# Row broadcasts as transposes, half of batch 0's weight quantising on VectorE, and new orders ahead of the experts

## The reference

```python
def _smooth_quant_linear(x, w):
    amax_x = jnp.max(jnp.abs(x), axis=0)
    amax_w = jnp.max(jnp.abs(w), axis=0)
    s = jnp.maximum(jnp.sqrt(jnp.maximum(amax_x, EPS) / jnp.maximum(amax_w, EPS)), EPS)
    xs, ws = x / s, w * s
    x_scale = jnp.maximum(jnp.max(jnp.abs(xs), axis=-1, keepdims=True), EPS) / QMAX
    w_scale = jnp.maximum(jnp.max(jnp.abs(ws), axis=-1, keepdims=True), EPS) / QMAX
    x_q = jnp.clip(jnp.round(xs / x_scale), -QMAX, QMAX)
    w_q = jnp.clip(jnp.round(ws / w_scale), -QMAX, QMAX)
    return x_q @ w_q.T * x_scale * w_scale.T
...
h = _smooth_quant_linear(xe, guw)                  # first layer "a"
gate, up = jnp.split(h, 2, axis=-1)
a = jax.nn.silu(gate) * up
return _smooth_quant_linear(a, dw)                 # second layer "b"
...
x = x + jnp.tanh(g_xattn[0]) * xattn(_layernorm(x), ...)
x = x + jnp.tanh(g_ffn[0]) * moe(_layernorm(x), ...)   # top 2 of 16, plus shared expert
```

## Time and profile before

| | us |
|---|---|
| median of 3 runs | 571.96 (571.3 to 572.04) |
| profiled execution | 572.15 |
| its span, first to last instruction | 570.1 |
| TensorE busy | 541.2 (95%) |
| VectorE busy | 419.4 (74%) |
| ScalarE busy | 331.3 (58%) |
| GpSimd busy | 155.4 (27%) |

### The profile page before, as it was taken

How to read it: one execution, slowest core, us unless ns; L and a number is a source line. 1 busy time by engine, 2 the same in 40 slices (tenths; PEclk the granted TensorE clock), 3 DMA queues, 4 the chain that set the end, 5 groups by cost and what they waited for, 6 DMA issues and landing times.

```text
span 570.1 us, 10175 instructions
## 1 busy us (share of the span) xinstructions
PE 541.2 (95%) x3768; PEld 459.9 (81%) x3776; DVE 419.4 (74%) x828; ACT 331.3 (58%) x570; POOL 155.4 (27%) x187
## 2 busy tenths in 40 slices
PE   7897879999999999999999999999999999999997
PEld 3453438986888788888889999999999999999985
DVE  3777988998899786587576666666666667765785
ACT  3286776686648627423466666666666667752221
POOL 3428790431033101103222111111111100066730
PEclk9989999999999999999999999999999999999999
DMA  7940121013001130113877776666677767556862
GB/s 265 386 145 2 37 107 43 2 38 147 1 2 38 75 102 2 68 57 88 270 254 251 254 241 225 226 225 225 228 237 254 247 216 249 176 160 188 261 216 75
DMA packets 45891, 89.52 MB, mean 157 GB/s; under 512 B 4304, under 2 KB 24784, under 8 KB 44832
## 3 DMA queue, kind: packets, MB, share of 16 engines
q1 hardware_dynamic: 40736, 72.26, 37.8%
q0 software_dynamic: 5120, 16.78, 9.2%
HBM read 72.25 MB, written 16.78 MB: 156 GB/s over the span
## 4 chain that ended last, share of the span: by engine, by line
PE 57%; DVE 23%; ACT 8%; POOL 6%; issue 5%; DMA 1%; DVEq 0%; SPq 0%; POOLq 0%; ACTq 0%
PE ps_gu L1866 9%; PE ps_gu L1867 9%; PE ps_gu L1868 9%; PE ps_d L1866 6%; PE ps_d L1868 5%; PE ps_d L1867 5%; PE ps_a L2120 3%; POOL w L492 2%; POOL sw_lo L508 2%; PE ps_gu L2427 1%; DVE bn_b L1101 1%; PE ps_d L1887 1%; DMA raw_gu<-in_L_ffn_w_up 1%; ACT y L760 1%; DVE x L1323 1%
## 5 line engine op out<-in xcount | busy, mean ns | idle before, releaser
L1866 PE MATMUL ps_gu<-ex_xhi,w_hi 128*128 128x256 f32 x352 | 99.5, 283 | 0.7 <-DVE wb L1461 0.5
L1867 PE MATMUL ps_gu<-ex_xlo,w_hi 128*128 128x256 f32 x352 | 99.5, 283 | 0.0
L1868 PE MATMUL ps_gu<-ex_xhi,w_lo 128*128 128x256 f32 x352 | 99.4, 282 | 0.0
L1866 PEld LDWEIGHTS ps_gu<-ex_xhi,w_hi 128*128 128x128 f32 x352 | 67.0, 190 | 3.3 <-issue 0.9
L1867 PEld LDWEIGHTS ps_gu<-ex_xlo,w_hi 128*128 128x128 f32 x352 | 67.1, 191 | 1.7
L1004 ACT ACTIVATE ex_hhi<-ex_hid 128x256 fp32r<-128x256 f32 (+1 forms) x66 | 27.6, 418 | 68.3 <-DVE ex_hid L1724 67.3
L1868 PEld LDWEIGHTS ps_gu<-ex_xhi,w_lo 128*128 128x128 f32 x352 | 67.1, 191 | 0.0
L1866 PE MATMUL ps_gu<-xt_hi,sw_hi 128*128 128x256 f32 x220 | 65.1, 296 | 0.1
L1867 PE MATMUL ps_gu<-xt_lo,sw_hi 128*128 128x256 f32 x220 | 62.0, 282 | 0.0
L1868 PE MATMUL ps_gu<-xt_hi,sw_lo 128*128 128x256 f32 x220 | 62.0, 282 | 0.0
L1866 PE MATMUL ps_d<-wd_hi,ex_hhi 128*128 128x512 f32 (+1 forms) x132 | 54.2, 411 | 1.4 <-DVE ex_hlo L1726 1.0
(11 more groups left out here) (255 smaller groups left out, 1386.7 us busy)
## 6 DMA issues: line engine op xcount, KB each, us to landing
raw_gu<-in_L_ffn_w_gate SPq DMA_DIRECT2D x16, 704.0 KB, 4.4
raw_gu<-in_L_ffn_w_up SPq DMA_DIRECT2D x16, 704.0 KB, 5.9
raw_d<-in_L_ffn_w_down SPq DMA_DIRECT2D x16, 512.0 KB, 7.2
expert_out_scratch<-eo SPq DMA_DIRECT2D x16, 512.0 KB, 7.3
w<-in_fside_BxS2xS SPq DMA_DIRECT2D x4, 1024.0 KB, 5.4
x2n_scratch<-y SPq DMA_DIRECT2D x4, 1024.0 KB, 3.9
x<-in_x SPq DMA_DIRECT2D x1, 3072.0 KB, 16.4
raw_d<-in_L_ffn_w_down SPq DMA_DIRECT2D x16, 192.0 KB, 7.3
```

The source lines that it names most:

```text
L1866: pe.matmul(dst, a_hi, b_hi, start=start, stop=False)
L1867: pe.matmul(dst, a_hi, b_lo, start=False, stop=False)
L1868: return pe.matmul(dst, a_lo, b_hi, start=False, stop=stop)
```

## The change

`row` uses four fp32 transposes instead of four fp32 matmuls. Batch 0's `quant_w` becomes `quant_w_first` on ScalarE (the first two groups of rows) and `quant_w_rest` on VectorE (the other two), with a semaphore of its own that `turn_qw(0, ...)` also waits for. All five lists have a new order ahead of the experts, and the fillers other counts. The same calls are made otherwise. The diff, cut to its core:

```diff
@@ SyncE
             load_w2(2)
+            store_x2n(1)
             load_w1(3)
-            store_x2n(1)
             load_w2(3)
@@ GpSimd
             scale_w(0)
+            norm_a(1)
+            norm_a(2)
             split_gu_lo(0)
-            norm_a(1)
-            split_gu_lo(1)
-            norm_a(2)
             root_b(0)
             scale_w2(0)
             root_a(1)
-            split_gu_lo(2)
             scale_w(1)
             split_d_lo(0)
+            split_gu_lo(1)
             norm_b(0)
             split_d_lo(1)
+            split_gu_lo(2)
             split_gu_lo(3)
@@ ScalarE
+            def quant_w_first(a):
+                act.wait_ge(w_steps_done[LA], a + 1)
+                for j in range(HALF):
+                    last = act.activation(w1[:, j, :], w1[:, j, :], ACT.Copy, bias=MAGIC + LOW16, scale=small[LA]["w_inv"][:, j:j + 1])
+                last.then_inc(qw_done[LA], 1)
...
             normalise_a(0)
-            tanh()
             copy_s(0)
             quant_x(0)
             ints_x(0, 0)
-            quant_w(0)
+            quant_w_first(0)
             ints_x(0, 1)
             copy_w(0)
             ints_w(0, 0)
             ints_w(0, 1)
+            split_d_hi(0)
             split_gu_hi(0)
             split_gu_hi(1)
-            router()
-            split_d_hi(0)
             silu_a(0)
             abs_w(1)
             normalise_a(1)
             abs_x(1)
             split_gu_hi(2)
             copy_sb(0)
+            tanh()
+            split_gu_hi(3)
             quant_g(0)
+            router()
+            copy_s(1)
+            ints_g(0)
             quant_w2(0)
-            ints_g(0)
             copy_wb(0)
-            copy_s(1)
             ints_w2(0)
             quant_x(1)
...
@@ VectorE
+            def quant_w_rest(a):
+                dve.wait_ge(w_steps_done[LA], a + 1)
+                for j in range(HALF, J):
+                    last = dve.tensor_scalar(w1[:, j, :], w1[:, j, :], small[LA]["w_inv"][:, j:j + 1], MAGIC + LOW16, ALU.mult, ALU.add)
+                last.then_inc(qw_rest_done, 1)
...
             w_steps(0)
+            quant_w_rest(0)
             stats_a(1)
+            amax_w2(0, 1)
             stats_a(2)
-            amax_w2(0, 1)
             dequant_a(0, 0)
...
             x_steps(1)
+            router()
+            w_steps(1)
             dequant_b(0, 0)
             dequant_b(0, 1)
             dequant_b(0, 2)
             dequant_b(0, 3)
-            w_steps(1)
             add_x(0)
             stats_b(0)
+            dequant_a(1, 0)
             stats_a(3)
...
@@ TensorE
             def row(dst, cols):
                 for c in range(C):
-                    last = pe.matmul(dst[:, c * P:(c + 1) * P], cols[:, c:c + 1].broadcast_to((P, P)), ident[:], start=True, stop=True)
+                    last = pe.transpose(dst[:, c * P:(c + 1) * P], cols[:, c:c + 1].broadcast_to((P, P)), ident[:])
...
                 pe.wait_ge(qw_done[LA], a + 1)
+                if a == 0:
+                    pe.wait_ge(qw_rest_done, 1)
...
             row_s(0)
-            keep_busy(23)
+            turn_w2(0, 1)
+            turn_router()
+            keep_busy(21)
             turn_qx(0, 0)
-            turn_router()
             turn_qx(0, 1)
+            keep_busy(1)
             row_w(0)
-            keep_busy(8)
+            keep_busy(6)
             turn_qw(0, 0)
-            turn_w2(0, 1)
             turn_qw(0, 1)
-            keep_busy(4)
+            keep_busy(5)
             product_a(0, 0)
...
             row_rs(1)
             keep_busy(1)
+            row_s(1)
             turn_qg(0)
             row_w2(0)
-            row_s(1)
+            keep_busy(8)
             turn_qw2(0)
...
             table(3)
+            shared_down(1, 1, 5, 1)
+            shared_up(2, 1, 5, 0)
             shared_down(2, 1, 0, 0)
             shared_down(2, 1, 0, 1)
             shared_down(2, 1, 1, 0)
-            shared_up(2, 1, 4, 1)
             shared_down(2, 1, 1, 1)
             shared_down(2, 1, 2, 0)
-            shared_up(2, 1, 5, 0)
             shared_down(2, 1, 2, 1)
```

More of the change, by code:

```diff
@@ L858, in _ @@
             x_hi(0, 3)
+            silu_a(1)
             abs_w(2)
-            silu_a(1)
             copy_logits(0)
+            normalise_a(2)
             shared_silu(0, 0, 0)
+            abs_x(2)
+            shared_hi(0, 0, 0)
             abs_g(1)
-            normalise_a(2)
             shared_silu(0, 0, 1)
-            shared_hi(0, 0, 0)
-            abs_x(2)
-            copy_sb(1)
             shared_silu(0, 0, 2)
             shared_hi(0, 0, 1)
+            copy_sb(1)
             quant_g(1)
@@ L873, in _ @@
             shared_silu(0, 0, 3)
+            copy_s(2)
             quant_w2(1)
-            copy_s(2)
             ints_g(1)
@@ L1483, in _ @@
             amax_w(0, 3)
+            amax_w2(0, 0)
             amax_x(0, 0)
@@ L1489, in _ @@
             smooth_a(0)
-            amax_w2(0, 0)
             scale_x(0)
@@ L1521, in _ @@
             dequant_b(0, 3)
-            w_steps(1)
             add_x(0)
             stats_b(0)
+            dequant_a(1, 0)
             stats_a(3)
-            dequant_a(1, 0)
             dequant_a(1, 1)
@@ L1658, in _ @@
             smooth_b(3)
-            shared_hid(1, 1, 0)
-            count(2)
             shared_hid(1, 1, 1)
-            shared_lo(1, 1, 0)
             scale_g(3)
@@ L2121, in turn_tokens @@
                 last.then_inc(ex_xt, 1)
-            keep_busy(23)
+            keep_busy(19)
             turn_w(0, 0)
@@ L2131, in _ @@
             turn_w2(0, 0)
+            keep_busy(4)
             turn_x(0, 0)
@@ L2164, in _ @@
             row_b(0)
-            keep_busy(2)
+            keep_busy(4)
             turn_peaks_x(1)
@@ L2205, in _ @@
             turn_peaks_w2(1)
+            turn_peaks_w(2)
             shared_up(0, 0, 1, 0)
-            turn_peaks_w(2)
             shared_up(0, 0, 1, 1)
+            shared_up(0, 0, 2, 0)
+            turn_peaks_x(2)
             turn_peaks_g(1)
-            shared_up(0, 0, 2, 0)
             shared_up(0, 0, 2, 1)
+            shared_up(0, 0, 3, 0)
             row_b(1)
-            shared_up(0, 0, 3, 0)
-            turn_peaks_x(2)
+            shared_up(0, 0, 3, 1)
             shared_down(0, 0, 0, 0)
-            shared_up(0, 0, 3, 1)
+            row_rs(2)
             shared_down(0, 0, 0, 1)
+            row_s(2)
             shared_up(0, 0, 4, 0)
-            row_rs(2)
+            turn_qg(1)
             shared_down(0, 0, 1, 0)
-            turn_qg(1)
-            row_s(2)
+            shared_up(0, 0, 4, 1)
             row_w2(1)
-            shared_up(0, 0, 4, 1)
+            shared_up(0, 0, 5, 0)
             turn_qw2(1)
             shared_down(0, 0, 1, 1)
-            shared_up(0, 0, 5, 0)
+            shared_down(0, 0, 2, 0)
             product_b(1, 0)
@@ L2263, in _ @@
             rank(0)
+            shared_up(0, 1, 4, 0)
             turn_peaks_w(3)
-            shared_up(0, 1, 4, 0)
-            shared_down(0, 1, 0, 0)
             shared_up(0, 1, 4, 1)
+            shared_down(0, 1, 0, 1)
             table(0)
@@ L2374, in _ @@
             shared_down(1, 1, 4, 1)
-            shared_up(2, 1, 2, 0)
+            shared_up(2, 1, 2, 1)
             rank(2)
-            shared_up(2, 1, 2, 1)
+            shared_up(2, 1, 3, 0)
+            shared_up(2, 1, 3, 1)
+            table(2)
             shared_down(1, 1, 5, 0)
-            shared_up(2, 1, 3, 0)
-            table(2)
             rank(3)
+            shared_up(2, 1, 4, 0)
+            shared_up(2, 1, 4, 1)
+            table(3)
             shared_down(1, 1, 5, 1)
-            shared_up(2, 1, 3, 1)
-            shared_up(2, 1, 4, 0)
-            table(3)
+            shared_up(2, 1, 5, 0)
             shared_down(2, 1, 0, 0)
```

360 lines of the change are left out of this document (180 added, 180 removed).

## The result

The changed kernel takes 568.87 us (median of 5 runs, 568.57 to 570.04) against 572.04 us before (571.3 to 573.82): a ratio of 0.9944, 95% interval 0.9932 to 0.9956. It is 3.2 us faster. The forecast was 563.0, 9.0 us faster, with a range from 559.3 to 567.2, so the direction was right and two thirds of the gain did not come. The profiled execution has a span of 566.5 us against 570.1, 3.6 us less.

A forecast was written before the change was run, and what follows sets the result against it. It took TensorE's work to bound 90 to 273 us and a chain of waits through all four engines the time before; 4.5 early plus 4.5 from rows made 9.0 us off, 563.0 us, range 559.3 to 567.2.

The forecast's parts named there:

- 12 x 0.45 = 5.4 us, if TensorE stays the bound ... I take 4.5: Shared expert stretch: 12 rows as transposes each give back 0.45 us of TensorE; taken as 4.5, between 0.5 and 7.
- Rival (a): Shared stretch no longer bound by TensorE, row time returns as waits for VectorE or ScalarE; 567.0 us, chance 0.17.
- Handing over: Between `table(3)` and `turn_tokens(0)`: first gathers have about 1 us less cover; plus and minus 0.6, taken as nothing.
- `load_w1(3)` behind the store: SyncE: load moves behind `store_x2n(1)`, lands 5.4 us later, perhaps up to 2 us late for `abs_w(3)`; taken as nothing.
- The early gain: Ahead of the shared expert, up to 90 us: shared expert starts 4.5 us earlier, between 3 and 5.5.
- The start: Batch 0's first scaling: rows as transposes bring the weight step's inverse from 30.1 to 29.2 us, 0.9 earlier.
- The split: Batch 0's weight quantising, half by VectorE at 0.42 us an operation: dequantisation starts 2.2 us earlier (1.8 to 2.6).
- The table: tanh moved behind `copy_sb(0)`: 3.0 us of loads and activations hidden in ScalarE's idle 4.59, none before `silu_a(0)`.
- rival (b): Early gain half lost, by GpSimd's splits before `norm_b(0)` or a load before `silu_a(0)` or `quant_g(0)`; 565.3 us, chance 0.13.
- GpSimd's order: Norms ahead of the splits, `split_gu_lo(1)` behind `scale_w(1)`: 0.8 and 1.3 us gained on top of 2.2 at `smooth_b(0)`.
- `norm_b(0)`: GpSimd: now behind five pieces of `split_d_lo(0)` and `split_gu_lo(1)`; no loss taken, up to 1.6 us.
- rival (d): Transposes do not hold TensorE's clock; slower only from eight falls on the chain, 572.6 us, 575 with ten; chance 0.04.

The follow-up runs named there:

- rows_only: The kernel before with its 20 rows as transposes and nothing else; 572.69 us beside 572.53, ratio 0.9997.
- rows_mm: The changed kernel with its rows as matmuls again; 574.83 us, ratio 1.0042.
- ve_half: The kernel before with two of VectorE's reductions of batch 2 over half the columns; 572.42 us beside 572.34, ratio 0.9992.
- combo_start: The changed kernel with tanh early, expert 1's load behind the first gather, 14 fillers ahead of `turn_y(0, 0)`, none of the four ahead of `turn_x(0, 0)`; 565.56 us, ratio 0.9884.
- split_only: The kernel before with half of batch 0's weight quantising moved from ScalarE to VectorE; 571.97 us beside 572.30, ratio 0.9992.
- tanh_early: The changed kernel with `tanh()` back behind `normalise_a(0)`; 568.68 us, ratio 0.9932.
- fill_y: The changed kernel with 14 fillers in place of 5 ahead of `turn_y(0, 0)`; 567.51 us, ratio 0.9906.

## Why the prediction was wrong

By landmarks 3.7 of the 9.0 us came. No one term holds the 5.3 that are missing: the shared stretch lacks 2.0, the early gain 2.3, the handing over 1.0.

**The step that failed** is "12 x 0.45 = 5.4 us, if TensorE stays the bound ... I take 4.5". The stretch gave 2.5 us up to the wait for the gather, and 0.7 with it. The row's saving was sized rightly (0.60 for 1.05 in the dense stretch, as in the earlier trace rows, and 0.65 for 1.16 behind a wait), and 4.1 us of work did leave TensorE's list. What failed was the bound: 1.6 of them came back as waits, mostly for VectorE and ScalarE. TensorE's 97% busy from 90 to 273 us was read as cause. In the kernel before, VectorE's waits in the first 46 us behind the logits sum to 1.3 us. Rival (a) named this, "a list shorter by 5.4 shows such chains more often", gave "only the early gain and some 0.5", and 567.0; its 0.5 is what the old order shows (rows_only, 0.4), and the new order kept 2.1 us more. The argument against it, "32 us of VectorE slack", was an average over 183 us: 21.6 of these 31.6 us lie behind 190 us. That rows_mm is 4.1 us slower in this stretch doesn't save the step: it shows that the new order was made for short rows. Without them, and without the wait for the gather, it would have been 1.6 us worse than the old one.

**Handing over**, "plus and minus 0.6, taken as nothing", is the second step that failed. The cover was as forecast: from `table(3)` to `turn_tokens(0)` 9.4 us of work instead of 10.4. But the load for expert 1 was issued 8.6 us earlier, not "some 4", and so ahead of the gather; a gather behind two loads took 7.0 us, without them at most 3.7, and `turn_tokens(0)` waits 1.85 us. Against that, expert 1's work began earlier, and a stall of 0.58 us in expert 0 is gone: from `turn_tokens(0)` to expert 1's `wb` matmul the changed kernel needs 13.1 us, 0.8 less than before. `load_w1(3)` behind the store: `abs_w(3)` waited 0.86 us for it, within the 0 to 2 held.

**The early gain**, forecast 4.5, was 2.2 at the logits. Against the forecast it lost 0.8 at the start, 1.25 for the table and 1.5 for the clock, and won some 1.2 in smaller terms:

- The start: the inverse ends at 30.0 instead of 29.2. The row's 0.9 came, and "I charge [fillers] nothing" was wrong by as much: four fillers stand ahead of `turn_x(0, 0)`, which moved from 13.66 to 14.56 (some 0.7 of it theirs, by all traces). In the one trace without them the inverse ends at 29.2.
- The split: 0.44 us an operation (forecast 0.42), and `dequant_a(0, 0)` at 37.04 (36.5, plus the 0.8 late start) as VectorE's list gave it. But what it was set against, 38.76, holds a fall at 30 us that is absent here; with like clocks the time from the inverse is 0.85 us shorter (8.05 in ve_half, 7.2 here), not 1.6. That part of the match is luck. The fall of the earlier trace rows, priced at 1.2 us by its eight fillers, cost some 0.75 on the chain.
- The table: "I take it that the first table loaded will then be Silu's" failed. The first load, at 5.74 for an Identity, is as before; Silu's came at its first use, on the chain, 1.28 us. That is rival (b) by its second mechanism, at half its price. The Trainium skill ("ScalarE: Activation LUTs", What ACT_TABLE_LOAD costs) gives 2.66 us for a switch, with a drain; the trace shows 1.28 us and the next activation 0.02 us behind it, and `gate_up(0)` comes 1.28 us sooner behind `dequant_a(0, 0)` without it, so it did not agree.
- GpSimd's order: right. `root_b(0)` gained 2.3 us on `gate_up(0)`, against 0.8 + 1.3.
- `norm_b(0)`: "I take no loss, up to 1.6"; it was 0.4.
- The clock: rival (d)'s mechanism, too small to turn the sign. One fall of 3.4 us cost 1.5 us between `turn_y(0, 0)` and the logits (6.4 us with it, 4.9 without, in every trace). The prediction asked for eight falls on the chain before it counted, and priced none in the forecast. But they are not all or nothing: the trace of the rows alone has two more than before, and its logits are no earlier.

With the start, the table and the clock mended, the trace of combo_start has the logits 5.5 us earlier than before, and 4.8 us counted from `turn_x(0, 0)` beside ve_half, which has no fall at 30 us. The 4.5 was there to be had.

The sum as measured: 2.2 early + 2.5 in the shared stretch - 1.85 for the gather + 0.8 behind it = 3.7, and 3.6 of span. The range ended at rival (a)'s 567.2; the kernel at 568.9 is half of rival (a), half of (b), one fall of (d) and the gather at once. Each was priced alone, with no case for two together, though their mechanisms were independent.

What stays open: how many falls of the clock an execution gets. They differ from run to run of one kernel. Why split_only and tanh_early show less in their medians than in their traces is not shown; their mean clocks (0.996 and 0.993) are a hint only. Which of the moves in the new order keeps the 2.1 us that the old one loses was not taken apart.

## What to carry to other kernels

An engine that is 97% busy need not be the one that sets the time. Before pricing a shorter instruction, follow the saved time to the next meeting point: who else must arrive there, and is that one earlier too? If not, little of the saving arrives until the order is searched again (here 0.4 us in the old order, 2.5 in the new). An order searched anew has to be read for what moved to the head of a chain: a first use of a function, a few fillers, a big load before a small gather. When rivals are independent, give a case to two of them together. And before a gain of one pair of traces is put down to an edit, look where each has its falls of the clock: one of them was worth 0.75 us at 30 us and 1.5 at 81.

## What the runs showed of the hardware

- Up to 280 us the half clock came in pieces of 3.4 us (6.8 in rows_mm, from 272 us, and in fill_y, from 267). The one at 81 us cost 1.5 us, the one at 30 some 0.75, the one at 53 in ve_half nothing that the landmarks show. Replacing 20 rows of matmuls by half as many transpose instructions, and nothing else, lowered the mean clock of the whole execution from 0.997 to 0.993.
- The activation table loaded for an Identity at 5.7 us served tanh (in tanh_early tanh runs at 13.33 with no load before it), and so did the one loaded for Silu. A load is 1.28 us; Silu's stands directly in front of the first Silu, wherever that is (13.5 or 40.6 us).
- TENSOR_SCALAR of 128x512 fp32 with a scalar per partition took 0.44 us on VectorE, where ScalarE takes 0.64 for the same, and VectorE's own tensor-tensor operations on that size 0.7.
- A gather issued behind two loads of 704 KB of expert weights released TensorE 7.0 us after its issue; without them in front it had landed at most 3.7 us after it.
